# A two-layer decoder on one core: mask in bf16 parts, ScalarE's function loads placed by hand, and the last stage's next context projected inside the self attention

## The reference

```python
# rotary embedding of stage a, on q and k (heads of 16)
q = q * c + rotate_half(q) * s        # rotate_half: [-q[8:], q[:8]] in each head
# stage d, first block
q = w8a8_linear(x, wq, bq)            # x and wq rounded to 127 steps of each row's largest value
k, v = cond @ wk.T + bk, cond @ wv.T + bv
scores = einsum('bhnd,bhld->bhnl', q, k) / 4 + mask[:, None]      # mask: 128x128 f32 per batch
o = softmax(scores) @ v
x = layernorm(x + w8a8_linear(o, wo, bo))
# stage d, second block
gating = softmax(x @ W_gate.T); head = argmax(gating)
k1, v1 = k[head], gating[head] * v[head]                          # one key and value head per row
x = layernorm(x + causal_attention(q, k1, v1))
```

## Time and profile before

| | |
|---|---|
| median of 3 runs | 2225.88 us (2225.17 to 2228.59) |
| profiled execution, its own time | 2224.3 us |
| its span in the trace | 2222.6 us |
| TensorE busy, share of the span | 1976.7 us, 89% |
| VectorE (DVE) busy | 1408.6 us, 63% |
| ScalarE (ACT) busy | 921.7 us, 41% |
| granted TensorE clock, mean over the span | 0.937 |

### The profile page before, as it was taken

The page is one execution under the profiler, slowest core; times in us unless marked ns, Lnnn a source line. Parts: engine busy times, 40 slices in busy tenths (PEclk is TensorE's granted clock), DMA queues, the critical chain, the costliest instruction groups (busy, mean ns, idle before and its releaser), DMA issues. The chain is left out here.

```text
span 2222.6 us, 27504 instructions
## 1 busy us (share of the span) xinstructions
PE 1976.7 (89%) x10158; PEld 1466.2 (66%) x10158; DVE 1408.6 (63%) x3232; ACT 921.7 (41%) x1661; POOL 80.2 (4%) x107
## 2 busy tenths in 40 slices
PE   6989998899994889998999999999999983999897
PEld 5878877555553557586675866758577672666665
DVE  3667655333222577877788677886877764657566
ACT  4455553211111544344453445445354422444454
POOL 0000000100002000000000000000000000000000
PEclk9999999899996899999999999999999996989899
DMA  3000000500002120202102021030111102000000
GB/s 139 6 15 10 6 6 7 199 1 10 1 0 86 35 50 11 56 22 48 39 15 54 29 39 39 15 62 22 38 40 31 37 1 76 8 13 15 8 5 6
DMA packets 132533, 72.19 MB, mean 32 GB/s; under 512 B 109809, under 2 KB 122673, under 8 KB 131409
## 3 DMA queue, kind: packets, MB, share of 16 engines
q1 hardware_dynamic: 132400, 70.44, 12.0%
HBM read 57.13 MB, written 13.11 MB: 32 GB/s over the span
## 5 line engine op out<-in xcount | busy, mean ns | idle before, releaser
L1357 PE MATMUL c_bank<-c_Y,c_NP 128*128 128x128 f32 x1536 | 187.8, 285 | 0.6 <-ACT c_Y L1509 0.6
L1357 PEld LDWEIGHTS c_bank<-c_Y,c_NP 128*128 128x128 f32 x1536 | 184.1, 201 | 4.1 <-issue 4.1
L1681 DVE TENSOR_TENSOR c_Y<-c_V,c_bank 128x512 f32<-128x512 f32 x192 | 131.9, 687 | 84.2 <-PE c_bank L1357 84.2
L1612 DVE SCALAR_TENSOR_TENSOR c_cv<-c_pad,c_wcqk,c_cv 128x1024 f32<-128x1024 f32 x96 | 122.3, 1282 | 9.7 <-ACT c_cv L1487 8.9
L1281 PE MATMUL c_bank<-c_xT,c_wqk 128*128 128x512 f32 x256 | 118.8, 608 | 9.1 <-ACT c_zs L1505 5.5
L1612 DVE SCALAR_TENSOR_TENSOR c_cv<-c_pad,c_wcv,c_cv 128x1024 f32<-128x1024 f32 x96 | 122.6, 1284 | 4.9 <-ACT c_cv L1487 2.3
L1655 DVE SCALAR_TENSOR_TENSOR c_NP<-c_NP,c_cj,c_bank 128x256 f32<-128x256 f32 x256 | 104.9, 476 | 27.4 <-ACT c_NP L1515 27.4
L1434 PE MATMUL c_bank<-c_wout,c_yT 128*128 128x256 f32 x512 | 121.2, 383 | 0.0
L899 ACT ACTIVATE b_sg<-b_G 128x512 f32<-128x512 f32 x50 | 29.7, 597 | 214.9 <-PE b_G L844 214.9
L1281 PE MATMUL c_bank<-c_xT,c_wv 128*128 128x512 f32 x256 | 111.2, 592 | 0.0
L1340 PE MATMUL c_bank<-c_wz,c_xT 128*128 128x512 f32 x256 | 111.2, 592 | 0.0
(11 more groups left out here) (413 smaller groups left out, 3947.9 us busy)
## 6 DMA issues: line engine op xcount, KB each, us to landing
b_wup<-b_in_wup SPq DMA_DIRECT2D x4, 1280.0 KB, 13.6
c_wqk<-c_in_wqk SPq DMA_DIRECT2D x9, 512.0 KB, 3.3
c_wv<-c_in_wv SPq DMA_DIRECT2D x8, 512.0 KB, 3.2
c_wz<-c_in_wz SPq DMA_DIRECT2D x8, 512.0 KB, 4.6
c_wout<-c_in_wout SPq DMA_DIRECT2D x8, 512.0 KB, 3.5
diagonal_blocks<-c_NP SPq DMA_DIRECT2D x64, 64.0 KB, 2.0
c_A<-diagonal_blocks SPq DMA_DIRECT2D x8, 512.0 KB, 3.7
c_NP<-no_blocks SPq DMA_DIRECT2D x32, 128.0 KB, 4.6
```

The source lines that it names most:

```text
L1357: last = pe.matmul(banks[n % 4][:, b * P:(b + 1) * P], lhsT(h, 4 * q + b), rhs(h, 4 * q + b), start=True, stop=True)
L1612: dve.scalar_tensor_tensor(cv[:, m % 2], pad[:, m % 2, :, t:t + S], w, cv[:, m % 2], ALU.mult, ALU.add)\
L1681: dve.tensor_tensor(rr(Y, h, q), rr(V, h, q), four(banks[n % 4][:, :]), ALU.subtract).then_inc(s["y_ready"], 1)
```

## The change

It has these parts, in stages a and d:

1. **Mask (d).** VectorE splits each 128x128 float32 mask in three parts: the upper 16 bits read as bf16, the same of the rest, and what then remains. TensorE adds them to the scores by three bf16 matmuls in place of one float32 matmul.
2. **Function loads (a and d).** `load_function` runs a 128x1 activation of Exp or Sqrt at chosen places, so that the table load stands there.
3. **Keys (d).** In the cross attention the keys of quad s + 1 are expanded ahead of step s's exp; in the self attention the two lanes' first quads come ahead of their second. In a, `EARLY` becomes (4, 1).
4. **Next context (d).** The context's transpose, the key projection and the value projection of round i + 1 move into steps 3, 4 and 5 of the self attention of round i; the copy of the context and the addition of key offsets likewise.
5. **Quantization (d).** The mask's splitting and the three parts of the input's quantization move to steps 0 to 3 of the self attention. `scale8` of the next round stands between the two parts of layer norm 2.
6. **Rotation (a).** The rows of q and k are permuted so that all first halves of heads lie in partitions 0 to 63 and all second halves in 64 to 127. The swapped projection goes; VectorE reads the other half's partitions instead (two half multiplications in place of one).
7. **Late work (a).** The end of layer norm 2 moves to step 2 of the next self attention, the window mask to its step 3.

```diff
+def load_function(act, scratch, function, done):
+    act.activation(scratch[:, 0:1], scratch[:, 1:2], function).then_inc(done, 1)
...
-        EARLY = (3, 1)
+        EARLY = (4, 1)
...
-                for r, bank in enumerate((L.M, L.S)):
-                    for n in range(4):
-                        for c in range(DC):
-                            last = pe.matmul(bank[:, n * P:(n + 1) * P], w["wqk"][:, r, c, n, :], L.xcT[:, c, :],
-                                             start=c == 0, stop=c == DC - 1)
+                for n in range(4):
+                    for c in range(DC):
+                        last = pe.matmul(L.M[:, n * P:(n + 1) * P], w["wqk"][:, c, n, :], L.xcT[:, c, :],
+                                         start=c == 0, stop=c == DC - 1)
...
                 for quad in range(EARLY[L.n]):
                     expand_keys(act, L.kexp[:, quad // 2], L.qk[:, 2 + quad // 2, :], own_block, quad, L.kexp_ready)
+                if L.n == 0:
+                    load_function(act, L.scratch, ACT.Exp, L.function_loaded)
...
                 L.ln1.on_scalar(act, i)
+                if L.n:
+                    load_function(act, L.scratch, ACT.Exp, L.function_loaded)
...
+            def rotate_halves(L, link):
+                link(dve.tensor_tensor(L.t1[:, :, :], four(L.M[:, :]), spread(w["rope"][:, 0, :], 4), ALU.mult),
+                     dve.tensor_tensor(L.t2[LOW, :, :], four(L.M[HIGH, :]), spread(w["rope"][HIGH, 1, :], 4), ALU.mult),
+                     dve.tensor_tensor(L.t2[HIGH, :, :], four(L.M[LOW, :]), spread(w["rope"][LOW, 1, :], 4), ALU.mult))
+                dve.tensor_tensor(L.qk[:, :, :], L.t1[:, :, :], L.t2[:, :, :], ALU.add).then_inc(L.qk_ready, 1)
...
-                yield from L.self_att.on_vector(dve, i)
+                for s, _ in enumerate(L.self_att.on_vector(dve, i)):
+                    if s == 2:
+                        for _ in L.last_norm:
+                            pass
+                    if s == 3:
+                        visible(i, L)
+                    yield
...
-                    pe.matmul(four(bank[:, :]), ident[:, :], spread(L.mask[:, :], 4), start=True, stop=False)
+                    for k, part in enumerate(mask_parts):
+                        pe.matmul(four(bank[:, :]), identb[:, :], spread(part, 4), start=k == 0, stop=False)
...
-                yield from L.self_att.on_tensor(pe, i, self_scores, self_values)
+                for s, _ in enumerate(L.self_att.on_tensor(pe, i, self_scores, self_values)):
+                    if more and s == QUADS - 1:
+                        transpose_context(i + 1, L)
+                    if more and s == QUADS:
+                        project_keys(i + 1, L)
+                    if more and s == QUADS + 1:
+                        project_values(i + 1, L)
+                    yield
...
+                if L.n:
+                    load_function(act, L.scratch, ACT.Exp, L.function_loaded)
                 yield
 
             def lane_program(i, L, more):
 
                 act.wait_ge(L.kT_ready, at(i, DC, DC))
-                for s, _ in enumerate(L.cross_att.on_scalar(act, i)):
-                    quad = s + 1
+                attention = L.cross_att.on_scalar(act, i)
+                for quad in range(1, QUADS + 2):
                     if quad < QUADS:
                         expand_keys(act, L.kexp[:, quad // 2], L.kT[:, quad // 2, :], own_block, quad, L.kexp_ready)
+                    next(attention)
                     yield
...
+            def part_mask(i, L):
+                dve.wait_ge(L.mask_loaded, at(i, 16, 16))
+                dve.tensor_tensor(L.mask_rest[:, :], L.mask[:, :], top_bits(L.mask[:, :]), ALU.subtract).then_inc(L.mask_parted, 1)
+                dve.wait_ge(L.mask_parted, at(i, 2, 1))
+                dve.tensor_tensor(L.mask_low[:, :], L.mask_rest[:, :], top_bits(L.mask_rest[:, :]), ALU.subtract).then_inc(L.mask_parted, 1)
...
+                next_input = quantize_input(i + 1, L) if more else iter(())
                 for s, _ in enumerate(L.self_att.on_vector(dve, i)):
-                    if more and s == 2:
-                        quantize_input(i + 1, L)
+                    if s < 5:
+                        next(next_input, None)
+                    elif more:
+                        add_key_offsets(i + 1, L)
                     yield
```

More of the change, by code:

```diff
@@ L669, in lane_program @@
                 dve.wait_ge(L.x2_free, i + 1)
-                yield from L.ln2.on_vector(dve, i, L.x2[:, :], L.x1[:, :], L.T[:, 0:D])
+                norm = L.ln2.on_vector(dve, i, L.x2[:, :], L.x1[:, :], L.T[:, 0:D])
+                next(norm)
+                yield
                 if more:
+                    L.last_norm = norm
                     yield from start_batch(i + 1, L)
+                else:
+                    next(norm, None)
+            for L in lanes:
+                L.last_norm = iter(())
             in_turns([start_batch(0, L) for L in lanes])
@@ L692, in layout_layer0_attention @@
     row = np.arange(P)
-    sign = np.where(row % HD < half, -1, 1).astype(f)[:, None]
+    sign = np.where(row < P // 2, 1, -1).astype(f)[:, None]
     root = f(0.5)
@@ L2133, in lane_program @@
                 act.wait_ge(L.krepT_ps, i + 1)
-                for quad in range(2):
-                    expand_keys(act, L.kexp[:, 0], L.M[:, 0:P], own_block, quad, L.kexp2_ready)
+                expand_keys(act, L.kexp[:, 0], L.M[:, 0:P], own_block, 0, L.kexp2_ready)
                 yield
-                yield from L.self_att.on_scalar(act, i)
+                expand_keys(act, L.kexp[:, 0], L.M[:, 0:P], own_block, 1, L.kexp2_ready)
+                for s, _ in enumerate(L.self_att.on_scalar(act, i)):
+                    if more and s == QUADS - 1:
+                        copy_context(i + 1, L)
+                    yield
+                if L.n:
+                    load_function(act, L.scratch, ACT.Sqrt, L.function_loaded)
                 yield
@@ L2141, in lane_program @@
                     return
-                next_start = start_batch(i + 1, L)
-                next(next_start)
-                yield
-                L.ln2.on_scalar(act, i)
-                yield from next_start
+                yield from start_batch(i + 1, L)
+            for L in lanes:
+                copy_context(0, L)
             in_turns([start_batch(0, L) for L in lanes])
@@ L2230, in lane_program @@
                 dve.wait_ge(L.xo_free, i + 1)
[L2231 removed]
+                norm = L.ln2.on_vector(dve, i, L.xo[:, :], L.x5[:, :], L.osb2[:, :, :].rearrange("p h d -> p (h d)"))
+                next(norm)
+                yield
                 if more:
[L2233 removed]
+                    scale8(i + 1, L, 0)
+                    yield
+                next(norm, None)
+                yield
             for L in lanes:
[L2236 to L2237 removed]
+                for _ in quantize_input(0, L):
+                    pass
+            for L in lanes:
+                add_key_offsets(0, L)
+            for L in lanes:
+                scale8(0, L, 0)
             for i in range(0, B // LANES - 1):
```

108 lines of the change are left out of this document (71 added, 37 removed).

## The result

The changed kernel takes 2191.01 us (median of 4 runs, 2187.15 to 2195.16), the kernel before 2227.24 us beside it (4 runs, 2225.17 to 2234.86): a ratio of 0.9843, with a 95% interval from 0.9816 to 0.9871. The prediction was 2192.6 us, 2178 to 2210. The profiled execution is the slowest of the four: 2195.16 us, span 2193.4 us.

A forecast was written before the change was run, and what follows sets the result against it. TensorE, busy over 84%, bounds stages a and d through idle time and half clock; 27.5 + 9.5 - 5 + 1.3 = 33.3 us less than 2224.3 gives 2191.0, expected median 2192.6 us, range 2178 to 2210.

The forecast's parts named there:

- Cross attention, 27.5 us: Stage d: new key order, moved load and bf16 mask save 7.5 us in rounds 1 to 3, some 5 in round 0.
- C to V: Stage d: cross attention's first mask matmul to its first value product; forecast 9.05 us in place of 15.9.
- rival 3: Stage d's cross-attention scores: reading every second bf16 is slow; at 0.8 us a matmul, 2249 us; chance 0.04.
- Moved loads, priced at nothing in stage d: Stage d: early Exp load delays `x5T`, but VectorE then finds gating's exp ready, so it costs nothing.
- Weighing the loads: Table loads: profile shows exp 0.02 us behind the load; the skill's 1380 ns draining was set aside for it.
- End of the self attention, 9.5 us: Stage d: projections inside steps 4 and 5 and spread quantization save 3.2 us, three times.
- C - E: Stage d: self attention's last value product to the next cross attention's start; forecast 7.2 us.
- Rival 1: Stage d's round end gives nothing: last steps at half clock slip 3 us; 2202 us; chance 0.17.
- Clock, -5 us: Stage d: uncovered idle time brings one half-clock loss of 1.64 us to each new cross attention.
- rival 2: Stages a and d: clock losses 11.5 us more, 2204 us, or fewer, 2182 us; together chance 0.10.
- Stage a, +1.3 us: Stage a: 4.0 us gained over four rounds, less 1.5 for the Exp load and 1.2 for the window mask.
- Stages b and c: The unchanged middle stages, 1459.3 us together, stay; moving by more than a few microseconds makes the forecast wrong.

The follow-up runs named there:

- the better version: Changed kernel without added function loads in stages a and d, three quads of keys first for lane 0, window mask again ahead of the rotation: 2184.02 us, ratio 0.9802.

## Why the prediction was right, and where not

The median came 1.6 us from the forecast. That closeness is in part luck: the cross attention, the end of the round, the clock and stage a were each off by 1 to 2.3 us, in both directions, and in the profiled pair stages b and c took another 5.1 us away.

**Cross attention, 27.5 us: right, 26.5.** C to V was to be 9.05 us and is 9.1 to 9.3. The three bf16 mask parts cost the 0.22 us each that I took from the bounds, and rival 3, that reading every second bf16 is slow, is out: the record lasts 0.387 us in the median (0.385 to 0.400), that of the closely packed part 0.377. The reason given for the gain was incomplete. I had it from the load's new place and the keys' new order together; the order alone gives 20.3 us, because it also lets the build's load run ahead. The moved loads were not needed.

**Moved loads, priced at nothing in stage d: wrong.** The step that failed is "VectorE then finds gating's exp ready: nothing". TensorE waits for `x5T` directly, 0.41 us a round, and 0.39 us of it are left at K. With what half clock adds, the loads cost 2.5 to 5.4 us by pairs.

**Weighing the loads: the row was right.** In all these traces the next activation starts 0.01 us behind the end of a load, if its data are there, and a load that waits for nothing 0.02 us behind the activation ahead. The Trainium skill ("ScalarE: Activation LUTs", "What ACT_TABLE_LOAD costs") has 1283 ns for the load, which agrees, and 1380 ns of draining with a switch, of which no run here shows anything.

**End of the self attention, 9.5 us: right in size, 11.8 us.** It is 2.9 us in rounds 1 and 2, where 3.2 stood, 5.7 in round 0, whose half clock was twice as long, and 0.3 in round 3. C - E is 7.2 us, as predicted, the idle time on `yb` 1.66 (1.8), and the mask's subtractions take 0.57 us a batch (0.6). Rival 1 is out: the last steps run at full clock. What the text did not see is that its comparison sets a new end at full clock against an old one at half clock, and that this, not the path, is nearly all of the gain. Its sum is also off by 0.6 us: steps 4 and 5 begun at 2035.7 and lasting 7.6 us end at 2043.3, not at 2042.7; they took 7.2 us, which made up for most of it.

**Clock, -5 us: wrong.** The step was to charge one fall of the clock to each new cross attention for the idle time uncovered ahead of it. That idle time is there, 1.66 us, and no fall follows: no cross attention of after has half clock from C to V. What the clock takes back is in the middle of the round, W to K: 3.7 us, 1.6 of them the loads' own. That this is near 5 us is chance. In all, half clock in stage d fell from 90.8 to 56.1 us, so the clock gave more than it took; that gain stands in the terms for the cross attention and the round's end. Of rival 2, neither the 11.5 us more of losses nor the whole gain down to 2182 us came.

**Stage a, +1.3 us: nothing measured.** The profiled pair has -0.5 us, stage a alone a ratio of 0.9999, and the spread of the span is 4 us. The terms came out close. Ahead of the first value product 3.56 us a round are gained and 1.6, 4.0, 2.3 and 2.3 given back at the keys, the load and half clock, which leaves the 4.0 us of the prediction. The load at layer norm 1 costs 0.46 a round where 0.37 was said. The window mask in step 3 costs 0.30 us a round, as said. This shows only between rounds that have no half clock from the first scores to the last value product. TensorE's first value product and its last group of them in such a round, round 1 before (10.38 us apart) and round 0 after (10.69):

```profile
138.67 0.96 PE L162 MATMUL a_O<-a_vaug,a_ptbuf 128*128 128x17 f32 x8
...
149.05 2.75 PE L162 MATMUL a_O<-a_vaug,a_ptbuf 128*128 128x17 f32 x24
```
```profile
48.19 0.96 PE L162 MATMUL a_O<-a_vaug,a_ptbuf 128*128 128x17 f32 x8
...
58.88 2.75 PE L162 MATMUL a_O<-a_vaug,a_ptbuf 128*128 128x17 f32 x24
```

To the end of the last it is 13.13 and 13.44 us, and 13.14 in the better version that has the mask ahead of the rotation again. Rounds 2 and 3 before have 12.30, but there the first value product came 1.7 us later after the scores, behind half clock, so they can't be set against 13.44. The 1.14 us expected of the better version came from that comparison.

**Stages b and c.** I had said that the forecast would be wrong if they moved by more than a few microseconds, and c moved by 7.1, with no instruction changed. That is not this change's work but a spread of the kernel (next but one section), and the sum of stages of the profiled pair (29.1 us) is short of the predicted 33.3 for this reason; stage d alone gave 34.7 where 32 stood.

**Readings that were loose.** VectorE is busy 59 and 62% of stages a and d, not half or less. Rival 3's 14 us set 0.43 us a matmul against the old mask's 0.86; against the forecast's 0.65 they are 20 us. Neither changes the sum.

## What to carry to other kernels

When an engine waits for two things in a row, look for what could run in the first wait: putting the keys ahead of the exp gave 20 of 35 us, and also freed the function load, which the build had behind a wait. Don't place loads by hand before seeing where the build's own ones lie; ahead of a copy that TensorE waits for, one costs what it was to save. Work given to an engine (the mask's subtractions) costs by the step in which it stands, so a part that is worth 9 us in one arrangement can be worth nothing in another. And before a stretch is set against another, look at the granted clock of both: a gain of 2.9 us a round that looked like a shorter path was nearly all a clock that no longer fell.

## What the hardware showed that I had not expected

Stage c runs the same instructions in all kernels here, and its span takes values from 1152.7 to 1162.1 us. Windows of the shortest and the longest (with one float32 mask matmul, with three quads first):

```profile
691.30:1844.00 1152.70, 1035.75 (x5285) 773.47 (x5300) 857.42 (x1742) 517.53 (x761) 52.77 (x49) 0.95 0.17 37
```
```profile
689.40:1851.50 1162.10, 1045.36 (x5285) 782.76 (x5300) 857.54 (x1742) 517.83 (x761) 52.79 (x49) 0.93 0.17 37
```

VectorE's and ScalarE's busy time hardly changes, TensorE's grows with the span and its granted clock falls. The time at half clock within stage c is 125.3 us in the first and 151.7 in the second, and 134.4 and 145.2 in two between them (1155.0 us with stage d alone changed, 1159.0 without loads in d). Each kernel has one profile, but the kernel before was timed in 47 executions beside the experiments, and they show the same of one unchanged program: 2214.56 to 2236.49 us, at a mean granted clock of 0.942 in the fastest and 0.930 in the slowest, and the two go together over all 47 (correlation -0.98). So one program's time spreads from execution to execution, and goes with the clock. That stage c's 9 us are this spread fits, but no kernel was profiled twice to show it. They are as much as most of the parts studied here, which is why parts were priced by the spans of their own stage; stage a moves by 4 us in the same way. What sets it in a given execution was not found.
